# Down-sampling on 64x64 tiles in half steps, with the accumulators of PSUM dealt out anew

## What is computed

```python
x   = x + sin(W[c,0] * xx + W[c,1] * yy + b[c])     # xx, yy: coordinates from -1 to 1
out = x + bias[c]
out = upsample2(out, 12 taps)        # along both axes: 256x256 -> 512x512
out = leaky_relu(out, 0.2) * sqrt(2)
out = downsample2(out, 12 taps)      # along both axes: 512x512 -> 256x256
```

## Time and profile before

| | before |
|---|---|
| median of 3 runs | 6572.96 us |
| profiled execution: its time | 6572.63 us |
| profiled execution: span | 6570.9 us |
| PE busy | 6509.3 us, 99% |
| DVE, ACT, POOL busy | 4002.7, 3980.8, 1303.7 us |
| granted clock of TensorE, mean | 1.000 |
| DMA, mean | 85 GB/s |

### The profile page before, as it was taken

The page is one execution under the profiler, slowest core; times in us unless marked ns, Lnnn a source line. Parts: engine busy times, 40 slices in busy tenths (PEclk is TensorE's granted clock), DMA queues, the critical chain, the costliest instruction groups (busy, mean ns, idle before and its releaser), DMA issues.

```text
span 6570.9 us, 361569 instructions
## 1 busy us (share of the span) xinstructions
PE 6509.3 (99%) x148480; PEld 6210.1 (95%) x148480; DVE 4002.7 (61%) x6218; ACT 3980.8 (61%) x7688; POOL 1303.7 (20%) x1041
## 2 busy tenths in 40 slices
PE   6999999999999999999999999999999999999999
PEld 6999999999999999999999999999999999999999
DVE  6666666666666666666666666666666666666665
ACT  4666666666666666666666666666666666666665
POOL 2111111111111111111111111111111111111111
PEclk9999999999999999999999999999999999999999
DMA  3222222222222222222222222222222222222222
GB/s 121 85 84 84 85 85 85 84 84 83 83 84 85 85 85 85 85 85 83 85 85 85 85 83 83 83 84 85 85 85 85 85 85 83 84 85 85 85 84 78
DMA packets 580065, 558.27 MB, mean 85 GB/s; under 512 B 40400, under 2 KB 574928, under 8 KB 580048
## 3 DMA queue, kind: packets, MB, share of 16 engines
q1 hardware_dynamic: 580048, 558.02, 27.2%
HBM read 278.94 MB, written 278.92 MB: 85 GB/s over the span
## 4 chain that ended last, share of the span: by engine, by line
PE 99%; DVE 1%; DMA 0%; SPq 0%; issue 0%; ACT 0%; DVEq 0%; POOL 0%; POOLq 0%
PE p_ps L433 34%; PE y_ps L449 32%; PE o_ps L433 15%; PE a_ps L449 14%; PE o_ps L459 3%; DVE up_band L377 0%; DVE angle L354 0%; DVE angle L352 0%; DVE phase L344 0%; ACT trig L258 0%; DVE trig_parts L361 0%; DVE angle L356 0%; DVE turns L348 0%; DVE turns L350 0%; DVE trig_parts L360 0%
## 5 line engine op out<-in xcount | busy, mean ns | idle before, releaser
L392 DVE SCALAR_TENSOR_TENSOR z<-y_ps,leak 128x512 f32<-128x512 f32 x4096 | 2629.3, 684 | 1749.8 <-ACT leak L278 1749.8
L278 ACT ACTIVATE leak<-y_ps 128x512 f32<-128x512 f32 x4096 | 2280.0, 623 | 2108.0 <-PE y_ps L449 2107.6
L449 PE MATMUL y_ps<-up_band,a_sb 64*128 64x138 f32 (+2 forms) x32768 | 2539.2, 282 | 1.4 <-ACT a_sb L271 1.3
L433 PE MATMUL p_ps<-down_band,z 128*64 128x68 f32 (+1 forms) x65536 | 2440.8, 227 | 1.7 <-DVE p_rows L400 1.7
L245 POOL TENSOR_TENSOR x_sum<-x_raw,f_sb 128x512 f32<-128x512 f32 x1024 | 1291.3, 1283 | 5235.6 <-ACT f_sb L264 5226.3
L433 PEld LDWEIGHTS p_ps<-down_band,z 128*64 128x64 f32 x65536 | 2156.2, 137 | 160.6 <-DVE z L392 1.0
L449 PEld LDWEIGHTS y_ps<-up_band,a_sb 64*128 64x128 f32 x32768 | 2163.4, 186 | 75.1 <-issue 1.5
L400 DVE COPY p_rows<-p_ps 128x512 f32<-128x512 f32 x2048 | 1416.2, 691 | 802.3 <-PE p_ps L433 699.1
L449 PE MATMUL a_ps<-up_band,x_sum 64*128 64x138 f32 (+2 forms) x16384 | 1306.6, 275 | 28.6 <-POOL x_sum L245 28.5
L433 PE MATMUL o_ps<-down_band,p_rows 128*64 128x68 f32 (+1 forms) x32768 | 1170.2, 224 | 0.8 <-DVE p_rows L400 0.8
L449 PEld LDWEIGHTS a_ps<-up_band,x_sum 64*128 64x128 f32 x16384 | 1132.9, 187 | 29.4 <-POOL x_sum L245 29.0
(11 more groups left out here) (28 smaller groups left out, 43.0 us busy)
## 6 DMA issues: line engine op xcount, KB each, us to landing
x_raw<-in_x_dram SPq DMA_DIRECT2D x1024, 256.0 KB, 3.1
out_dram<-o_out SPq DMA_DIRECT2D x1024, 256.0 KB, 2.5
f_rows<-trig_dram SPq DMA_DIRECT2D x512, 20.0 KB
trig_dram<-trig_parts SPq DMA_DIRECT2D x32, 256.0 KB, 2.5
trig_dram<-ones SPq DMA_DIRECT2D x4, 256.0 KB, 2.4
trig_dram<-bias_wide SPq DMA_DIRECT2D x4, 256.0 KB, 2.5
up_taps<-in_L_conv_up_filter_dram SPq DMA_DIRECT2D x1, 6.0 KB, 2.3
down_taps<-_L_conv_down_filter_dram SPq DMA_DIRECT2D x1, 6.0 KB, 2.4
```

The lines of the kernel that those rows point to most:

```text
L278: nc.scalar.mul(leak[i % 2][:, :], y_ps[i][:, :], SLOPE * GAIN).then_inc(leak_done, 1)
L392: nc.vector.scalar_tensor_tensor(z[n][:, i, :], y_ps[i][:, :], GAIN, leak[i % 2][:, :], ALU.mult, ALU.max).then_inc(z_done, 1)
L433: last = nc.tensor.matmul(out_ps[half * HALF:(half + 1) * HALF, lo:hi], data[:, t, col:col + HALF], down_band[:, band:band + hi - lo], sta ...
L449: last = nc.tensor.matmul(outs[o][:, lo:hi], data[row, k, (at + o) * P:(at + o + 1) * P], up_band[row, band:band + hi - lo], start=step == ...
```

## The change

Both down passes go over to 64x64 tiles. One function `step_of` now issues every half step, up or down. A down half step goes over the four blocks of 128 rows of its data, over the upper and the lower 64 rows of each, which write to different banks, and over two column halves; the bands are 36 to 40 columns wide. p therefore has two banks (`p_ps[0]`, `p_ps[1]`), each of which takes half of the columns of both pairs, and is copied when all of p is done, one bank by ACT (`copy_p0`), one by DVE (`copy_p1`). o shares the two banks of a. f is made in y_ps[0] and y_ps[1], from three float32 rows (sine, cosine, bias) held twice, at partitions 0 and 64 of a cleared tile, by four 64x64 matmuls; DVE copies it in two halves (`copy_f`). a is copied half by ACT (`copy_a0`), half by DVE (`copy_a1`); o in two halves by ACT.

Each step begins with `pe.sem_inc(steps_begun, 1)`, behind its waits. PE's loop turns once a channel. At the start the tables are no longer split in two parts, and a round saves 4 DMAs in place of 10. The order of the loops:

```diff
+            def step_of(cols, outs, data, band, spans, at, where, ks, step, fresh=True):
+                pe.sem_inc(steps_begun, 1)
+                for k in ks:
+                    for rows in range(2):
+                        o = rows ^ step
+                        row = slice(rows * HALF, (rows + 1) * HALF)
+                        lo, hi, start = spans[k][rows]
+                        for part in range(0, P, cols):
+                            col = (at + o) * P + part
+                            last = nc.tensor.matmul(outs[o][part:part + cols, lo:hi], data[row, where[k], col:col + cols],
+                                                    band[row, start:start + hi - lo],
...
+            def sines(c, z_from):
+                pe.wait_ge(f_rows_loaded, 32 * c + 32)
+                reached(pe, z_done, z_from)
+                pe.sem_inc(steps_begun, 1)
                 for t in range(HT):
+                    row = slice(t * HALF, (t + 1) * HALF)
+                    for part in range(0, P, DOWN_COLS):
...
# PE, one slot
                 if y:
+                    up_cols(m, n, 0, 0, c + 2 if n == 0 and f_before else None, m + 1 if first else None)
                     up_cols(m, n, 1, 0)
                 if a_next:
+                    up_rows(m + 1, 1 - n, 0, first)
+                if y:
+                    up_cols(m, n, 0, 1)
+                if a_next:
                     up_rows(m + 1, 1 - n, 1)
                 if y:
                     up_cols(m, n, 1, 1)
                 if p:
+                    down_rows(m - 1, 1 - n, 0, 0)
+                    down_rows(m - 1, 1 - n, 0, 1)
                 if o:
+                    down_cols(m - 2, n, 0, m + 2 if a_next else None)
                 if p:
+                    down_rows(m - 1, 1 - n, 1, 0)
+                if o:
+                    down_cols(m - 2, n, 1)
+                if f_next and n == 1:
+                    sines(c + 2, 4 * m + 2)
+                if p:
+                    down_rows(m - 1, 1 - n, 1, 1)
...
# DVE, one slot
+                if a_next:
+                    copy_a1(m + 1, 1 - n)
                 if y:
                     leaky(m, n, 0)
                     leaky(m, n, 1)
+                if f_next and n == 1:
+                    copy_f(c + 2)
                 if y:
                     leaky(m, n, 2)
                     leaky(m, n, 3)
                 if p:
+                    copy_p1(m - 1, 1 - n)
...
# ACT, one slot
                 if y:
                     leaky(m, 0)
+                if a_next:
+                    copy_a0(m + 1, 1 - n)
+                if y:
                     leaky(m, 1)
                     leaky(m, 2)
                     leaky(m, 3)
+                if o:
+                    copy_o(m - 2, n, 16 * (c - 1))
+                if p:
+                    copy_p0(m - 1, 1 - n)
```

More of the change, by code:

```diff
@@ L71, in filtered_lrelu_kernel @@
         coord = sb("coord", [CP, H])
[L72 removed]
+        ones = sb("ones", [CP, H])
         phase = sb("phase", [CP, 4, H])
@@ L206, in step @@
                         store(c - 1, n)
+                if more_rows:
+                    sp.wait_ge(f_made, c + 3)
+                    load_f_rows(c + 3)
             step(0, True, True, stores=False)
-            with sp.Fori(1, C - 2) as c:
+            with sp.Fori(1, C - 3) as c:
                 step(c, True, True)
+            step(C - 3, False, True)
             step(C - 2, False, False)
@@ L257, in _, with copy_a0 @@
                 act.wait_ge(angle_ready, t + 1)
[L258 to L266, removed]
+                nc.scalar.activation(trig[:, bass.ds(t, 1), :, :].rearrange("p t q n -> p (t q) n"), angle[:, :, :],
+                                     ACT.Sin).then_inc(trig_ready, 1)
+            def copy_a0(m, n):
                 act.wait_ge(a_made, m + 1)
                 reached(act, y_made, 4 * m - 4)
-                for t in range(HT):
-                    last = nc.scalar.copy(a_sb[n][:, t, :], a_ps[t][:, :])
-                last.then_inc(a_copied, 1)
+                nc.scalar.copy(a_sb[n][:, 0, :], a_ps[0][:, :]).then_inc(a0_copied, 1)
             def leaky(m, i):
@@ L412, in slot @@
                 if p:
[L413 removed]
+                    copy_p1(m - 1, 1 - n)
+            copy_f(0)
+            copy_a1(0, 0)
+            copy_f(1)
             slot(0, 0, p=False)
             slot(0, 1)
[L417 to L419 removed]
+            with dve.Fori(1, C - 2) as c:
                 slot(c, 0)
                 slot(c, 1)
[L422 removed]
+            slot(C - 2, 0)
+            slot(C - 2, 1, f_next=False)
+            slot(C - 1, 0)
+            slot(C - 1, 1, a_next=False, f_next=False)
+            slot(C, 0, a_next=False, y=False)
         @block.tensor
         def _(pe):
[L426 to L442 removed]
+            def step_of(cols, outs, data, band, spans, at, where, ks, step, fresh=True):
+                pe.sem_inc(steps_begun, 1)
+                for k in ks:
                     for rows in range(2):
@@ L445, in up @@
                         row = slice(rows * HALF, (rows + 1) * HALF)
-                        lo = max(0, 256 * k + 128 * rows - 6)
-                        hi = min(UP, 256 * k + 128 * rows + 132)
-                        band = lo + 6 - 256 * k
-                        last = nc.tensor.matmul(outs[o][:, lo:hi], data[row, k, (at + o) * P:(at + o + 1) * P],
-                                                up_band[row, band:band + hi - lo], start=step == 0 and k == 0,
-                                                stop=step == 1 and k == HT - 1, skip_group_check=True)
@@ L499, in slot, with down_rows @@
-            def slot(c, n, a_next=True, f_next=True, y=True, p=True, o=True, f_done=None):
+                    step_of(P, outs, a_sb[n], up_band, UP_SPAN, 2 * pair, range(HT), range(HT), 1).then_inc(y_made, 2)
+            def down_rows(m, n, step, pair):
+                if step == 0:
+                    if pair == 0:
+                        pe.wait_ge(z_done, 4 * m + 4)
+                        reached(pe, p0_copied, m)
+                        reached(pe, p1_copied, m)
+                elif pair == 0:
+                    pe.wait_ge(p_half, m + 1)
+                last = step_of(DOWN_COLS, [p_ps[o][:, pair, :] for o in range(2)], z[n], down_band, DN_SPAN, 2 * pair,
+                               range(UT), range(UT), step, pair == 0)
+                if pair == 1:
+                    last.then_inc(p_made if step else p_half, 1)
```

261 lines of the change are left out of this document (119 added, 142 removed).

## The result

The changed kernel takes 7143.68 us (median of 4 runs, 7141.5 to 7146.12) against 6572.96 us: 1.0868 times as long, with a 95% interval of 1.0849 to 1.0887. The forecast was 6930 us in a range of 6650 to 7500. The sign, the place and the mechanism were right; the size was 214 us short: 571 us were lost where the forecast had 357.

What follows compares the result with a forecast made beforehand. PE's list bounds the kernel. A channel of 5.76 + 5.54 + 1.98 + 0.12 = 13.40 us against 12.69 gives +363 over 512 channels, less 5 at the start: 6930 us, range 6650 to 7500.

Steps and rivals of the forecast that it cites:

- The wait for f: PE at y pair 0 behind sines, waiting for DVE's copy of f: 0.59 us lost a channel.
- the wait for z: PE at y pair 1, waiting for two DVE leaky operations that stand behind the copy of f: 0.74 us a channel.
- S: The end of sines on PE, from which the forecast counts; y pair 0 at S + 1.24, y pair 1 at S + 2.44.
- a plain slot: An item's stretch of PE's list without sines: six up steps, six down steps and changes of shape, 5.76 us.
- The tiles: Down passes on four 64x64 tiles at once, bound by weight loads: 0.44 us a half step, gain 0.27 us an item.
- `steps_begun`: 25 more instructions a channel in PE's list, carrying the waits: 0.01 us for each of 12 down steps, 0.12 a channel.
- two tiles at a time: Rival, down passes: only two tiles run at once, 27.5 ns an instruction, kernel 9350 us; chance 0.10.
- a floor per matmul: Rival, down passes: matmul starts at least 25 ns apart engine-wide, kernel 8900 us; chance 0.10, shared with two tiles at a time.
- changes of shape: PE's two switches of tile shape an item, between up and down steps: they stay, 0.36 us.
- The slot with sines: The item's stretch of PE's list that holds sines: 5.54 us to S, and 1.98 us on.
- The loop's turn: PE's loop, turning once a channel in place of once in two: no gap, costs nothing.
- The start and the end: Ahead of the first copy of f, table rounds lose a copy and a subtraction, 2.0 us each: 5 us taken off.

Runs made afterwards that it cites:

- Experiment 1: Changed kernel with DVE's leaky operations on y_ps[2] and y_ps[3] put ahead of the copy of f: 6766.53 us, 1.0296 times the kernel before.
- experiment 4: Changed kernel with both down passes back on 128x64 tiles and bands of 68 and 72 columns: 7280.43 us.
- Experiments 5 and 6: Changed kernel with down bands of 32 columns, 7137.19 us; changed kernel with 32 stationary columns in place of 64 in each down matmul, 6721.76 us.
- experiment 3: Changed kernel without the sines of channels 2 to 511, their copies and loads: 6274.79 us.
- experiment 8: Changed kernel with sines a step earlier and ACT copying f: PE's loop over two channels a turn, 10559.11 us; its turn moved into the up steps, 6465.51 us.

## Why the prediction was right, point by point

- **The wait for f and the wait for z** were the deciding step, and held: predicted 0.59 and 0.74 us a channel. The prediction named the step, the releasers and the cause, and the times behind sines came out within 0.03 us each. With S at 3003.65, the first MATMUL behind sines, the copy of f started 0.37 us behind it for 0.35, its two halves took 0.76 for 0.78, DVE to PE 0.14 for 0.11, and y pair 1 started at S + 2.46 for S + 2.44. Experiment 1 gives the second wait 0.73. Without any wait y pair 0 would have come 0.58 behind S (a plain slot's last p step, 3010.99 to 3011.57) and not 0.65, so the first wait costs 1.27 - 0.58 = 0.69.
- **The tiles**: four at once, bound by their stationary columns and not by the band, 0.44 us a step predicted and 0.467 measured. The row behind the 55 ns was the head of a step, where a load has nothing to wait for; running on, a set of four takes 58. Over the 11 down steps ahead of S in the two slots that is 0.30 us a channel. The sum had 0.12 apart from this for `steps_begun` in the down steps, so 0.18 of the 0.36 by which the channel was short (13.76 for 13.40) are this; the rest is in the next point. The gain of the tiles was put at 0.27 us an item and is 0.16 (experiment 4: 0.31 a channel). Experiments 5 and 6 show that it is the 64 stationary columns, and neither the band nor the number of instructions. The rivals of two tiles at a time and of a floor per matmul are out: PE's MATMULs start 0.467 / 32 = 14.6 ns apart on the mean. The 25 ns of the Trainium skill (TensorE: Matmul & The Clock Gate, "Wait — 56ns, not 53.3ns?") do not hold here for the engine as a whole; for one tile, with a MATMUL every 58 ns, they are not tested.
- **A plain slot**: 5.76 predicted, 5.92 measured, of which 0.16 are the six down steps. The two changes of shape an item stayed at 0.35 us. **The slot with sines** reached S after 5.84 us for 5.54: five down steps account for 0.13; 0.10 is my error, for of the 0.21 us that I took off for the change of shape behind S, half lies behind the first y step, at the head of the slot (two y steps take 1.02 us there, 3011.57 to 3012.59, in place of 0.92); 0.06 is a gap ahead of sines, 0.53 us from the step before it in place of 0.47; sines itself took 0.45 for 0.43.
- **steps_begun**: 0.12 predicted for the down steps; 0.09 measured for the up steps, at the waits. For those on the new tiles' down steps there is no run without them. On the old tiles there is: a down step takes 0.487 us with one (experiment 4, a mean of three steps) and 0.485 without (half of 0.97), so there it costs next to nothing.
- **The loop's turn**: priced at nothing, which was right for the changed kernel only because the wait for f covers it. Where no wait covers it, it is 0.23 us (experiment 3); with the copy of f beside it, 0.11 to 0.16 (experiment 8).
- **The start and the end** were the term with the wrong sign: -5 us predicted. Outside 512 channels of its pattern the kernel before spends 6570.9 - 512 x 12.70 = 68.5 us, the changed one 7143.1 - 512 x 13.762 = 97.0, with 13.762 the mean over 480 channels of its trace: +28. Two things were missed. A round of tables lost only 0.24 us and not 2.0 (from sine to sine 49.38 - 40.45 = 8.93 us, where it was 49.74 - 40.57 = 9.17). ACT now loads its table behind the wait for the angle, in the path, which is 1.28 of the missing 1.76 us; the rest I can't place. The changed kernel:

```profile
39.16 1.28 ACT L256 ACT_TABLE_LOAD   x1 [6.60 <-DVE angle L348]
40.45 1.06 ACT L256 ACTIVATE trig<-angle 128x1024 f32 x1
...
49.38 1.06 ACT L256 ACTIVATE trig<-angle 128x1024 f32 x1
```

The kernel before, where the load stood ahead of the wait:

```profile
32.45 1.28 ACT L258 ACT_TABLE_LOAD   x1
40.57 1.06 ACT L258 ACTIVATE trig<-angle 128x1024 f32<-128x1024 f32 x1 [6.83 <-DVE angle L356]
```

And PE's list has to be fetched for the first time just there, in the channels ahead of the loop and in its first turn, and again at the end. It is used up faster than before, for a down step is 64 instructions in 0.467 us. The changed kernel's timeline:

```profile
82.46 0.37 PE L449 MATMUL a_ps<-down_band,p_rows 64*64 64x40 f32 x10 [1.38 <-issue]
...
102.46 0.32 PE L449 MATMUL a_ps<-down_band,p_rows 64*64 64x40 f32 x6 [1.55 <-issue]
...
106.28 1.15 PE L449 MATMUL a_ps<-up_band,x_sum 64*128 64x132 f32 x8
...
7121.33 0.43 PE L449 MATMUL p_ps<-down_band,z 64*64 64x40 f32 x13 [2.02 <-issue]
```

Gaps of 0.8 to 2.0 us with no other engine to blame stand among them, and behind most of them up steps at half the clock, 0.90 us (106.28 to 107.18, granted clock 0.50). The trace bears out that these gaps are fetches. The queue that loads instructions moves one packet of 16 KB that starts between 80 and 81 us, one between 99.6 and 100 and one between 7118.7 and 7119, each 2.4 to 2.8 us ahead of the matmul that ends a gap, and none between 3000 and 3100. The kernel before moves 14 such packets in place of 19 and has no gap of this kind behind 60 us.

Experiment 4 divides the 28 us. Its kernel differs from the changed one in the down tiles alone, with half as many matmuls in a down step, and spends 7278.4 - 512 x 14.076 = 71.3 us outside its pattern. So 26 of the 28 us come with the doubled number of instructions, and the tables and all else account for about 3.

The sum, then: 512 x (13.762 - 12.70) = 544 us and 28, together 572, against 363 - 5.

## What to carry to other kernels

When one buffer takes over a second use, ask for each engine's list what stands behind the operation that frees it: here an in-order copy that waited 1.6 us blocked two operations that were ready, and cost more than new tiles gave. The same change with that copy on another engine and the loop's turn under queued work is 1.6% faster than the kernel before in place of 8.7% slower, and 2.4% faster when the up steps lose their semaphore instruction too. Of small tiles, price the stationary columns, most likely the weight load, as well as the band; of more instructions, price the first fetch of the list too: it took 26 of the 161 us that the tiles gave.

## What the runs showed of the hardware that was not expected

- Four 64x64 float32 tiles run at once: 32 MATMULs and 32 loads in 0.467 us with 64 stationary columns, in 0.31 us with 32, and the 0.467 are unchanged when the band goes from 39 to 32 columns.
- A loop twice as long on PE made the channel 20.5 us in place of 12.6 (mean over 480 channels), with 37.68 MB of instructions fetched against 0.31 MB.
- PE's loop turn costs 0.23 us when the array's work ahead of it is short matmuls and the next step waits on nothing, and nothing seen when up steps are queued ahead of it.
- In the channels ahead of the loop PE stood still for 1.2 to 1.6 us behind packets on the queue that loads instructions, and then ran at a granted clock of 0.50 for a while; a list with half as many matmuls in its down steps spent 26 us less at the start and the end.
- A semaphore wait on an instruction ahead of the weight load is met 0.09 us later than one on the load itself (0.14 us behind DVE's end, and 0.05).
